# A Swin block and a separable convolution on one core: softmax first in the step and MLP last, the first norm one strip further ahead

## What is computed

```python
xn = layer_norm(x); windows = roll(xn, (-3, -3)) cut in 7 x 7
q, k, v = windows @ qkv_w + qkv_b
attn = softmax(q * scale @ k.T + bias + mask)
x1 = x + roll_back((attn @ v) @ proj_w + proj_b)
y = x1 + gelu(layer_norm(x1) @ fc1_w + fc1_b) @ fc2_w + fc2_b
z = depthwise_3x3(relu(y)) + dw_bias
out = batch_norm(z @ pw_kernel + pw_bias)
```

## Time and profile before

| what | us |
|---|---|
| median of 3 runs | 6379.06 (6376.44 to 6382.61) |
| profiled execution | 6393.57 |
| its span, first to last instruction | 6391.8 |
| TensorE busy | 5565.9 (87%) |
| VectorE busy | 5516.4 (86%) |
| ScalarE busy | 5303.2 (83%) |
| GpSimd busy | 3803.8 (60%) |
| mean granted TensorE clock | 0.994 |

### The profile page before, as it was taken

How to read it: one execution, slowest core, us unless ns; L and a number is a source line. 1 busy time by engine, 2 the same in 40 slices (tenths; PEclk the granted TensorE clock), 3 DMA queues, 4 the chain that set the end, 5 groups by cost and what they waited for, 6 DMA issues and landing times.

```text
span 6391.8 us, 202888 instructions
## 1 busy us (share of the span) xinstructions
PE 5565.9 (87%) x81186; PEld 3984.3 (62%) x81186; DVE 5516.4 (86%) x13773; ACT 5303.2 (83%) x10784; POOL 3803.8 (60%) x4105
## 2 busy tenths in 40 slices
PE   5888888888888888888888888888888888888887
PEld 3666666666666666666666666666666666666665
DVE  4888888888888888888888888888888888888887
ACT  4888888888888888888888888888888888888886
POOL 2666656666666565655666666566666666566663
PEclk9999999999999999999999999999999999999998
DMA  0111111111111111111111111111111111111110
GB/s 22 27 33 31 31 32 29 33 28 33 28 33 28 33 28 33 29 33 28 33 28 33 28 33 28 33 30 31 32 29 33 28 33 28 33 28 33 30 31 22
DMA packets 275644, 193.69 MB, mean 30 GB/s; under 512 B 229159, under 2 KB 246040, under 8 KB 274712
## 3 DMA queue, kind: packets, MB, share of 16 engines
q1 hardware_dynamic: 274712, 180.70, 10.9%
HBM read 77.81 MB, written 77.07 MB: 24 GB/s over the span
## 4 chain that ended last, share of the span: by engine, by line
POOL 37%; PE 32%; DVE 17%; ACT 9%; issue 3%; SPq 1%; DVEq 0%; DMA 0%; POOLq 0%; ACTq 0%
PE bank L427 15%; POOL xn L944 13%; POOL prob L928 13%; POOL rstd L934 6%; PE bank L511 5%; DVE stats L838 5%; ACT L562 5%; POOL x1n L944 5%; PE bank L408 4%; DVE x L874 4%; PE bank L496 3%; PE bank L523 3%; DVE ssum L798 2%; ACT hT L616 2%; ACT prob L562 2%
## 5 line engine op out<-in xcount | busy, mean ns | idle before, releaser
L822 DVE SCALAR_TENSOR_TENSOR acc<-ymap,taps,acc 96x784 f32<-96x784 f32 (+2 forms) x2176 | 2562.1, 1182 | 45.7
L934 POOL TENSOR_TENSOR rstd<-var_eps,minus_half 112x7 f32<-112x7 f32 x512 | 936.1, 1828 | 2376.7 <-DVE var_eps L853 2376.7
L427 PE MATMUL bank<-x1T,w 96*128 96x448 f32 (+1 forms) x3072 | 1094.3, 506 | 1.9 <-ACT x1T L605 1.9
L446 PE MATMUL bank<-hT,w 128*96 128x448 f32 (+1 forms) x3072 | 1095.8, 492 | 0.0
L616 ACT ACTIVATE hT<-bank,bfc 128x448 f32<-128x448 f32 (+1 forms) x1536 | 883.8, 587 | 175.4 <-PE bank L427 118.3
L944 POOL TENSOR_SCALAR xn<-x_in,minus_mean,rstd 112x96 f32<-112x96 f32 x768 | 853.3, 1121 | 0.0
L928 POOL TENSOR_TENSOR prob<-prob,srec 128x392 f32<-128x392 f32 x768 | 803.3, 1075 | 82.4 <-DVE srec L800 82.4
L919 POOL TENSOR_TENSOR prob<-prob,smax 128x392 f32<-128x392 f32 x768 | 804.3, 1076 | 23.3 <-DVE smax L791 23.3
L427 PEld LDWEIGHTS bank<-x1T,w 96*128 96x128 f32 x3072 | 568.3, 192 | 394.8 <-issue 294.2
L446 PEld LDWEIGHTS bank<-hT,w 128*96 128x96 f32 x3072 | 465.9, 163 | 341.5 <-issue 163.5
L463 PE MATMUL bank<-ident,prob 113*113 113x113 f32 x3072 | 478.1, 278 | 228.0 <-POOL prob L928 220.7
(11 more groups left out here) (99 smaller groups left out, 10777.2 us busy)
## 6 DMA issues: line engine op xcount, KB each, us to landing
out<-o_tile SPq DMA_DIRECT2D x256, 210.0 KB
x_in<-in_x SPq DMA_DIRECT2D x256, 168.0 KB, 3.0
x_in<-in_x SPq DMA_DIRECT2D x256, 126.0 KB, 3.3
k<-qk SPq DMA_DIRECT2D x512, 49.0 KB, 1.9
out<-o_tile SPq DMA_DIRECT2D x256, 84.0 KB
hT<-in_L_conv_rel_bias SPq DMA_DIRECT2D x49, 0.6 KB
x1T<-in_L_conv_fc_w SPq DMA_DIRECT2D x1, 144.0 KB, 2.3
w<-in_L_conv_fc_w SPq DMA_DIRECT2D x1, 144.0 KB, 2.3
```

The costliest lines, as they stand in the source:

```text
L427: pe.matmul(bank[(5, 6, 0)[m]][:, 0:n * PT_], w1[:, m * 128:(m + 1) * 128], x1T[:, first * PT_:(first + n) * PT_], start=True, stop=True). ...
L446: mm = pe.matmul(bank[b][0:C, 0:n * PT_], w2[:, m, :], hT[:, m, first * PT_:(first + n) * PT_], start=False, stop=(m == MC - 1))
L822: last = dve.scalar_tensor_tensor(out=dst, in0=src, scalar=taps[:, i:i + 1], in1=dst, op0=ALU.mult, op1=ALU.add)
L934: pool.tensor_tensor(b["rstd"][:], b["var_eps"][:], minus_half[0:PT_], ALU.pow)\
```

## The change

The order of each engine's step is rewritten. On TensorE both halves of `pointwise` come ahead of `turn_x1`; `turn_probs` and `weigh_values` come ahead of the MLP; `project` lies between the halves of `hidden`, and `turn_x` between the halves of `second_layer`. On ScalarE the exps come right behind `queries` and `keys`, the gelu table is loaded behind `probs_turned`, `attention_out` is ahead of `gelus`, the exp table is brought in by a 1x1 activation behind the gelus, and then follow `normalise(0, t + 3)`, `into_map` half 0, `x_turned`, `normalise(1, t)` and `into_map` half 1. On VectorE the sums of the softmax follow one tap and the copies of the values; `norm_x` is behind `add_x` and works on strip t + 3; taps 7 and 8 are last. On GpSimd the roots and rests of both norms follow `shift` and `divide`. The first norm runs one strip further ahead, so xn is held twice; the second norm is scaled in its own strip's step, one earlier, and x1 is held twice. SyncE loads strip t + 4, behind the other DMAs of the step. The banks are shared out anew, and the waits with them. The steps begin at -3.

```diff
@@ -135,8 +135,8 @@
         x_in = sb("x_in", PT_, 4, WS, C)
-        xn = sb("xn", PT_, WS, C)
-        x1 = sb("x1", PT_, WS, C)
+        xn = sb("xn", PT_, 2, WS, C)
+        x1 = sb("x1", PT_, 2, WS, C)
         x1n = sb("x1n", PT_, WS, C)
         o_tile = sb("o_tile", HW, 2, WS, C)
         xT = sb("xT", C, TOK)
...
@@ -235,12 +235,12 @@
                 sp.dma_start(dst, src.rearrange("(u f) -> u f", u=1)).then_inc(rows_loaded, 16)
             def load(t, phase):
-                s = t + 3
+                s = t + 4
                 if not has(s):
                     return
-                slot = (phase + 3) % UNROLL
-
-                wait(sp, x1_ready, nth(t - 1, 2, 1))
+                slot = phase
+
+                wait(sp, x1_ready, nth(t, 2, 1))
                 image, k = s // NWIN, s % NWIN
                 first = (image * HW + k * WS + SHIFT) * NWIN
                 wrapped = (image * HW + (k + 1) % NWIN * WS) * NWIN
...
@@ -271,10 +271,11 @@
                     sp.dma_start(k0[b:b + HD, :], qk[a:a + HD, u * HALF:(u + 1) * HALF]).then_inc(k0_moved, 16)
             def step(t, phase):
-                load(t, phase)
                 move_keys(t)
                 store(t, phase)
-
+                load(t, phase)
+
+            load(-4, 0)
             load(-3, 1)
             load(-2, 2)
             sp.wait_ge(dve_set, 6)
...
@@ -331,9 +332,8 @@
                 wait(pe, q_ready, nth(t, 2, 1))
                 wait(pe, k_copied, nth(t, 1, 0))
                 wait(pe, k0_moved, 32 * (t + 1))
-                wait(pe, pt_ready, nth(t - 1, 3, 0))
-                wait(pe, ymap_ready, nth(t - 2, 2, 0))
-                wait(pe, out_ready, nth(t - 5, 2, 1))
+                wait(pe, o_ready, nth(t - 1, 1, 0))
+                wait(pe, h_ready, nth(t - 2, 6, 5))
                 def score(g, w):
                     u = w // PAIRS
...
@@ -370,9 +370,9 @@
                     return
                 wait(pe, xt_ready, nth(t + 1, 2, 1))
                 for u in range(2):
+                    wait(pe, ymap_ready, nth(t - 2, 2, u))
                     pe.matmul(bank[3 + u][:, 0:HALF], wqk[:, u, :], xT[:, u * HALF:(u + 1) * HALF],
                               start=True, stop=True).then_inc(q_psum, 1)
-                wait(pe, x1_ready, nth(t - 1, 2, 0))
                 for u in range(2):
                     mm = pe.matmul(bank[5][64 * u:64 * u + 64, 0:HALF], wk12[:], xT[:, u * HALF:(u + 1) * HALF],
                                    start=True, stop=True)
...
@@ -381,16 +381,13 @@
             def values(t, i):
                 if not has(t + 1):
                     return
-                if i == 0:
-                    wait(pe, ymap_ready, nth(t - 2, 2, 1))
-                else:
-                    wait(pe, q_ready, nth(t + 1, 2, 0))
+                wait(pe, xt_ready, nth(t + 1, 2, i))
                 for q in range(2 * i, 2 * i + 2):
                     for side in range(2):
                         for odd in range(2):
                             w = 4 * q + 2 * odd + side
                             at = (2 * (q % 2) + side) * C
-                            mm = pe.matmul(bank[(7, 3)[i]][64 * odd:64 * odd + NT, at:at + C],
+                            mm = pe.matmul(bank[6 + i][64 * odd:64 * odd + NT, at:at + C],
                                            xT[:, w * NT:(w + 1) * NT], wv[:], start=True, stop=True)
                 mm.then_inc(v_psum, 1)
...
@@ -417,29 +416,26 @@
                     if m == 0:
                         wait(pe, x1t_ready, nth(t - 1, 2, 1 - half))
                     if i == 0:
-                        wait(pe, k_copied, nth(t + 1, 1, 0))
+                        wait(pe, s_biased, nth(t, 3, 1))
                     elif i == 1:
-                        wait(pe, x1_ready, nth(t - 1, 2, 1))
-                    elif i == 2:
                         wait(pe, x1t_ready, nth(t - 1, 2, 0))
-                    else:
+                    elif i > 2:
                         wait(pe, h_ready, nth(t - 1, 6, i - 3))
-                    pe.matmul(bank[(5, 6, 0)[m]][:, 0:n * PT_], w1[:, m * 128:(m + 1) * 128],
+                    pe.matmul(bank[(1, 2, 5)[m]][:, 0:n * PT_], w1[:, m * 128:(m + 1) * 128],
                               x1T[:, first * PT_:(first + n) * PT_], start=True, stop=True).then_inc(h_psum, 1)
             def second_layer(t, half):
                 if not has(t - 1):
                     return
                 first, n = ((0, 4), (4, 3))[half]
-                b = (1, 7)[half]
+                b = (3, 4)[half]
                 if half == 0:
-                    wait(pe, x1t_ready, nth(t - 1, 2, 1))
-                    wait(pe, x1_ready, nth(t - 1, 2, 1))
+                    wait(pe, pt_ready, nth(t, 3, 2))
                 else:
-                    wait(pe, v_ready, nth(t + 1, 2, 0))
-                    wait(pe, ymap_ready, nth(t - 2, 2, 1))
+                    wait(pe, o_ready, nth(t, 1, 0))
+                wait(pe, out_ready, nth(t - 4, 2, half))
                 for a in range(n):
-                    pe.matmul(bank[b][0:C, a * PT_:(a + 1) * PT_], x1[:, first + a, :], ident[0:PT_, 0:PT_],
+                    pe.matmul(bank[b][0:C, a * PT_:(a + 1) * PT_], x1[:, (t - 1) % 2, first + a, :], ident[0:PT_, 0:PT_],
                               is_transpose=True, start=(a == 0), stop=False)
                 for m in range(MC):
                     wait(pe, h_ready, nth(t - 1, 6, 3 * half + m))
...
@@ -468,7 +465,9 @@
             def weigh_values(t, phase, g):
                 if g == 0:
                     wait(pe, v_ready, nth(t, 2, 1))
-                    wait(pe, h_ready, nth(t - 1, 6, 4))
+                    wait(pe, out_ready, nth(t - 4, 2, 1))
+                    if not has(t - 4):
+                        wait(pe, q_ready, nth(t + 1, 2, 1))
                 wait(pe, pt_ready, nth(t, 3, g))
                 for q in range(QUADS):
                     for side in range(2):
...
@@ -487,28 +486,26 @@
                     return
                 wait(pe, xn_ready, nth(t + 2, 1, 0))
                 wait(pe, xn_rest, nth(t + 2, 1, 0))
-                for i, (js, perm, b) in enumerate(((range(3, 7), ident[0:PT_, 0:PT_], 3), (range(0, 3), roll[:], 4))):
-                    wait(pe, pt_ready, nth(t, 3, i + 1))
-                    wait(pe, q_ready, nth(t + 1, 2, i))
-                    wait(pe, v_ready, nth(t + 1, 2, 1))
-                    wait(pe, out_ready, nth(t - 4, 2, 0))
+                for i, (js, perm, b) in enumerate(((range(3, 7), ident[0:PT_, 0:PT_], 6), (range(0, 3), roll[:], 7))):
+                    wait(pe, x1_ready, nth(t, 2, i))
+                    if t < 0:
+                        wait(pe, v_ready, nth(t + 1, 2, i))
                     for a, j in enumerate(js):
-                        mm = pe.transpose(bank[b][0:C, a * PT_:(a + 1) * PT_], xn[:, j, :], perm)
+                        mm = pe.transpose(bank[b][0:C, a * PT_:(a + 1) * PT_], xn[:, t % 2, j, :], perm)
                     mm.then_inc(xt_psum, 1)
             def pointwise(t, phase, i):
                 if not has(t - 4):
                     return
                 first, n = HALVES[i]
-                if not has(t):
-                    wait(pe, out_ready, nth(t - 5, 2, i))
                 if i == 0:
                     wait(pe, tap_done, nth(t - 4, 9, 8))
-                    wait(pe, q_ready, nth(t + 1, 2, 1))
-                else:
-                    wait(pe, s_biased, nth(t, 3, 2))
+                wait(pe, q_ready, nth(t + 1, 2, i))
+                if not has(t + 1):
+                    wait(pe, ymap_ready, nth(t - 2, 2, i))
+                    wait(pe, out_ready, nth(t - 5, 2, i))
                 for a in range(n):
-                    mm = pe.matmul(bank[(4, 2)[i]][0:HW, a * C:(a + 1) * C], acc[:, phase % 2, first + a, :], wpw[:],
+                    mm = pe.matmul(bank[3 + i][0:HW, a * C:(a + 1) * C], acc[:, phase % 2, first + a, :], wpw[:],
                                    start=True, stop=True)
                 mm.then_inc(pw_psum, 1)
...
@@ -530,20 +527,20 @@
                 queries_keys(t)
                 values(t, 0)
                 values(t, 1)
+                pointwise(t, phase, 0)
+                pointwise(t, phase, 1)
                 turn_x1(t)
-                pointwise(t, phase, 0)
-                hidden(t, 0)
-                hidden(t, 1)
-                second_layer(t, 0)
-                second_layer(t, 1)
                 if has(t):
                     for h in range(HEADS):
                         turn_probs(t, h)
                     for h in range(HEADS):
                         weigh_values(t, phase, h)
+                hidden(t, 0)
+                project(t)
+                hidden(t, 1)
+                second_layer(t, 0)
                 turn_x(t)
-                pointwise(t, phase, 1)
-                project(t)
+                second_layer(t, 1)
             steps(pe, step)
...
```

(105 more changed lines are left out.)

32 lines of the change are left out of this document (15 added, 17 removed).

## The result

The changed kernel takes 8466.49 us (8456.81 to 8469.1) against 6377.75 before (6373.88 to 6382.61): a ratio of 1.327, interval 1.325 to 1.330. It is slower, as forecast, but by 2089 us and not by 3200.

A forecast was written before the change was run, and what follows sets the result against it. Hand-overs between three nearly full engines bound the kernel, 24.41 us a step. The new ring of waits at TensorE's lower clock, 36.9, gave (36.9 - 24.41) x 256 = 3197 us more: 9580 us, range 7550 to 10040.

The forecast's parts named there:

- the ring: Waits through all four engines, once per step, via the late first norm: 29.4 us at upper clock, 36.9 at lower.
- the wait of ScalarE: ScalarE idle ahead of the first norm's scaling, until GpSimd's offset: 5 us or more per step.
- the gap of TensorE: TensorE idle ahead of the first queries, waiting for the x_turned copies: 5.0 us per step.
- GpSimd's part (i): GpSimd's root, offset, rest(1) and root(0) up to the first norm's scale: 6.2 us, between 4.7 and 6.9.
- ScalarE's tail (j): ScalarE's five operations from the first norm's scaling to into_map half 1: 6.7 us from start to start.
- The fall of the clock: TensorE's clock was to fall to the lower level in the gap ahead of the queries in every step.
- The return of the clock: TensorE's clock was to come back only in the middle of the projection, at 21.7 us of the turn.
- Step (g): TensorE's hidden tiles, then projection: at the lower clock 4.5 us of tiles, projection through at 21.7.
- the forecast period of 36.9: Length of one step with the ring at the lower clock, 36.9 us, bounds 35.1 to 38.7.
- rival B: Clock falls but returns before weigh_values in many steps: period 32 to 35.1, 8320 to 9110 us; chance 0.20.
- The table load (e): Gelu table load and small activation on ScalarE, behind the turned probabilities' copies, counted on the ring: 1.5 us.
- Rival D: ScalarE finds the norm's scale ready when gelus end; TensorE's order decides: 23.4 us a step, 6120 us; chance 0.04.

The follow-up runs named there:

- e1: Changed kernel with the first norm's statistics, root and rest put back early on VectorE and GpSimd, ScalarE's order left: 6390.15 us, ratio 1.0007.
- e4: Changed kernel with ScalarE's order alone altered, the first norm's scaling last in the step, behind into_map half 1: 6340.43 us, ratio 0.994.
- e6: Changed kernel with seven extra 384-column matmuls between scores and queries and two more between the pairs of query matmuls: 7962.12 us, ratio 1.247.
- e5: Changed kernel with the alterations of both e1 and e4: 5933.03 us, ratio 0.930.
- e8: e4 with one extra 384-column matmul ahead of the third group of turned probabilities: 6102.71 us, ratio 0.956.
- e10: e1 with one extra 384-column matmul between the two pairs of query matmuls: 6101.72 us, ratio 0.957.
- e11: e4 with seven small matmuls ahead of the third group of turned probabilities: 6125.21 us, ratio 0.960.
- e9b: e4 with 19 small matmuls ahead of the third group of turned probabilities: 6414.83 us, ratio 1.007.

## Why the prediction was right or wrong

- **The direction and the ring: right.** Its members, the wait of ScalarE and the gap of TensorE (5.0 forecast, 4.87 measured) are in the profile; taking the norm out of it (e1) or its tail away (e4) takes the whole loss away. Its length at the upper clock was summed as 29.4 and is 29.28 in e6.
- **GpSimd's part (i): right.** From the root's start to the scale is 4120.05 to 4126.22, 6.2 as forecast; `rest(1)` beside the taps takes 2.64, forecast 2.7.
- **ScalarE's tail (j): nearly.** 4126.30 to 4132.64, 6.3 for 6.7.
- **The fall of the clock: right.** It comes in nearly every step, in the gap, and two levels are all that is seen. "TensorE: Matmul & The Clock Gate", section "HAM oscillation — how this bites in real kernels" in the Trainium skill tells of a kernel whose clock falls again in each wait between bursts of matmuls. This trace agrees: 259 stretches for 256 strips.
- **The return of the clock: wrong, and nearly the whole error.** Step (g) at the lower clock put it into the projection, by the one long stretch of the earlier trace rows, and so charged turned probabilities, weighing and hidden tiles at the slow durations. They ran at the fast ones: 1.86, 1.66 and 2.36 from start to start, against the 2.71, 2.91 and 4.5 of the sum. These are 4.2 us of the 4.4 between the forecast period of 36.9, which the prediction named as a sign of being right, and the 32.5 of the mean step. Put as a price, the lower clock was to cost 36.9 - 29.4 = 7.5 us a step and costs about 3.2. The slow stretch before them was sized rightly (queries and keys 2.97 for 2.85, values 2.7 for 2.7). It was rival B, given 0.20, that came, near its lower end of 32 to 35.1; that the time lies inside the stated range is due to that rival.
- **The table load (e): its length right, its place not on the ring.** In the changed kernel it begins at 4112.47, lasts 1.28, and the small activation starts at 4113.77. But the copies behind it are through at 4115.36, and the projection starts at 4115.78 behind TensorE's own hidden tiles, so the chain doesn't pass through it. "ScalarE: Activation LUTs", section "What ACT_TABLE_LOAD costs" in the Trainium skill, adds a drain of 1.38; no run here shows it. The prediction let this drain lengthen the ring by 1.4; by its own sum, with `attention_out` at 12.05 and the hidden tiles at 12.3, an estimate is 1.1.
- **Rival D's condition: right in kind.** With ScalarE's wait off the ring the new order makes 23.3 us a step at the upper clock (e1, e4), as its 23.4 said. With both, e5 makes 22.6, so 23.4 was not the floor of TensorE's order.

## What to carry to other kernels

A new order is priced by its longest ring of waits, one turn per step, and not by busy shares: an operation whose input is made late in the same step is best the last thing on its engine, for whatever stands behind it joins the ring. If the ring leaves TensorE idle for microseconds in each step, add it up at the lower clock too, but take the return of the clock as a range, since the lower clock alone was about two fifths of the price here. Where a short wait costs the clock, work that nothing needs, put into the wait, can be worth more than it costs, and removing the wait is worth more still.

## What was not expected of the hardware

Waits of about 1 us were enough to let the clock fall: 1.00 in e1 and 0.89 in e4, in steps where TensorE has 21.5 us of work in 23.3 and no other wait over about 0.4 us. That gave 94 stretches at the lower clock in e1 (923 us) and 73 in e4 (657 us). e8, e10 and e11 show that filling the wait is enough, as each has 6 stretches in all.

The wait alone doesn't decide it. The kernel before has waits as long in every step (0.89 ahead of the third group of turns, 1.09 ahead of `turn_x`, 0.90 ahead of the turns of the norm, around 4111 to 4124 us), and its clock stays up through hundreds of steps: of its 7 stretches 2 lie between 200 and 6200 us. It has other matmuls between these waits, with the MLP right ahead of the turned probabilities; whether that order would keep the clock in the new kernel was not tried. e9b, with 1.8 us of small matmuls in the place of the wait and none over about 0.4 us left, still had 25 stretches, which no run here explains: the same length of wide work was not tried there. Why the clock came back after 10 to 17 us in each step of the changed kernel, and only after 20 in the stretch at 3009 us before, stays open too.
